# Decoder block in one kernel: where self-attention's exp and row sums, the rounding factors and the layer norms are computed

## The chip, the cores and the metric

The kernel runs on one core of a Trainium2 chip. The metric is the device time of one execution in microseconds (us), lower is better; the median of 3 runs is given. The engines are named as in the profile: PE is TensorE (matmuls and transposes; PEld is its loading of weights), DVE is VectorE, ACT is ScalarE, POOL is GpSimd, SP issues DMAs. Each engine takes its own instructions strictly in the order of its queue and waits on semaphores; SBUF is the on-chip memory, PSUM the eight banks into which PE writes.

## What is computed

A decoder block over x of shape (8, 256, 256): 8 batch elements of 256 tokens, width 256. Three parts follow one another, each with a layer norm ahead and a residual add behind:

```
x = x + attention(layernorm(x))              # causal, 8 heads of 128, 2 latent KV groups of width 32
x = x + cross_attention(layernorm(x), ctx)   # 16 heads of 16 over 77 context tokens, then relu MLP 256-512-256
x = x + ffn(layernorm(x))                    # two "bit linear" layers 256-1024-256 with exact gelu between

def bitlinear(x, w, b):
    xn = x * rsqrt(mean(x**2) + 1e-6)
    scale = 127 / clip(max(abs(xn)), 1e-5)             # per token
    xq = clip(round(xn * scale), -128, 127) / scale
    wq = ternary weights, scaled by mean(abs(w))
    return xq @ wq.T + b
```

In self-attention the probabilities are softmax(q k / sqrt(128)) with a causal mask, per head.

## The kernel before

The kernel works batch element by batch element (i = 0 to 7, on lines that the profile shows as counts of 8), each of two tiles of 128 tokens. For each element the same steps run, in groups: `sp` (layer norm, transposes and projections for self-attention), `sa` (scores, softmax numerators), `so` (weighted sum, output projection, residual), `xp`, `xs`, `xo`, `xm` (the same for cross-attention and its MLP), `f1` and `f2` (the two quantised layers), and `pro`, the one-time preparation of weights.

The work of several elements overlaps, and every engine's order is written out by hand: the table `ORDER` lists the steps of each engine, the calls at the end of each engine's function repeat it, and `Steps` turns a step's place into the semaphore count to wait for. PSUM has two uses. Four of its eight banks form `quad`, one single buffer for scores; each fill of it (self-attention's first query tile "A" with 128 keys, its second "B" with 256 keys, cross-attention's two tiles) must be emptied before the next fill. The other four are a ring that all other results of PE pass through, in PE's order.

Self-attention for one element, before:

- PE fills quad with the scores of 8 heads (`sa_scores`, L1784 to L1789; all heads share 32-wide latent keys, in 4 row groups and 2 columns c).
- DVE takes the negated maximum (`sa_max`, L1225) and adds it to the scores on the way to `a_sA` or `a_sB` in SBUF (`sa_sub`, L1235). This empties quad.
- PE transposes the differences (`sa_tr`, L1804: 2 banks for A, 4 for B), and ACT applies exp with the score's scale as it copies them to `a_p` (`sa_exp`, L821).
- PE computes the weighted sum with the values and, by a second set of matmuls with a tile of ones, the row sums spread over 32 rows (`so_pv`, L1822).
- DVE turns the sums: a stream transpose in blocks of 32 (L1244), a reciprocal of 8 columns (L1246), a transpose back (L1248), then the product (`so_y`, L1251). PE projects it (L1730) and DVE adds the residual (L1255).

A layer norm before takes its statistics on DVE (L1200, L1203), the inverse deviation on POOL (L518, L520), and on POOL also the normalisation, two instructions of 128x256 (`normalise`, L526). A rounding factor (`f1_quant`, `f2_quant` on POOL) is 127 over the guarded maximum: after DVE's maximum (L1325, L1350) POOL multiplies it by the inverse root mean square, clamps it, takes the power -1 and multiplies again (L568 to L575, L609 to L617), and DVE rounds with the factor (L1331, L1357).

ACT also applies gelu and exp from different tables: where it changes between them, a table load stands in its queue (ACT_TABLE_LOAD).

## Time and profile before

| | |
|---|---|
| median of 3 runs | 319.96 us (319.79 to 321.28) |
| the profiled execution | 321.1 us |
| its span, first to last instruction | 319.2 us |
| mean granted TensorE clock | 0.984 of full speed |
| DMA | 12.54 MB, nearly all in the first 33 us |

The profile gives for each engine the time in which it had an instruction under way ("busy"), and for each idle gap what ended it. An idle gap of an engine that sets no one's pace costs nothing; so the views by stretch of time and by group of instructions are read together. PE's matmuls overlap, so the busy time of a group is less than its count times the mean duration of one, and the pace is the distance from one to the next.

### The profile page before, as it was taken

The page shows a single profiled execution, that of the slowest core. Times are in us where ns is not written, and L with a number is a line of the kernel's source. Part 1 is how long each engine was busy: PE and PEld are TensorE (multiplying, and loading weights), DVE is VectorE, ACT ScalarE, POOL GpSimd, SP SyncE. Part 2 cuts the span into 40 slices and gives each one's busy share as a digit, 9 for nine tenths or more (in the row PEclk, how much of TensorE's full clock was granted, in tenths as well). Part 3 has the DMA queues.
Part 4 walks back from the last instruction along what each step waited for, and adds up shares of the span by engine and source line. Part 5 has one row for each costly group of instructions (what it writes and reads, how often), then busy time and mean ns, then how long its engine had stood idle before and what let it go on. Part 6 is the DMA issues. An engine that isn't in the chain of part 4 may idle for free.

```text
span 319.2 us, 8883 instructions
## 1 busy us (share of the span) xinstructions
PE 302.6 (95%) x3185; PEld 248.8 (78%) x3198; DVE 273.2 (86%) x488; ACT 191.0 (60%) x369; POOL 161.5 (51%) x315
## 2 busy tenths in 40 slices
PE   8798999999999999999999999999999999998756
PEld 8476787879888887897788878887887888786534
DVE  2228996898989799999999999989999998999973
ACT  3164435436247759478966854497445965776852
POOL 7337006282933523671778266306660485077873
PEclk9899999999999999999999999999999999999978
DMA  7999000000000000000001010000000010000011
GB/s 200 340 368 330 6 3 0 2 2 0 4 2 2 3 0 2 3 0 2 2 3 34 3 35 2 2 0 4 16 18 2 2 37 2 0 3 33 3 34 66
DMA packets 11954, 12.54 MB, mean 39 GB/s; under 512 B 1668, under 2 KB 11144, under 8 KB 11912
## 3 DMA queue, kind: packets, MB, share of 16 engines
q1 hardware_dynamic: 10648, 11.40, 10.9%
q10 hardware_dynamic: 1264, 0.59, 0.7%
q8 instruction: 26, 0.43, 0.6%
q14 instruction: 16, 0.13, 0.1%
HBM read 9.89 MB, written 2.10 MB: 38 GB/s over the span
## 4 chain that ended last, share of the span: by engine, by line
PE 77%; issue 6%; DVE 6%; POOL 5%; ACT 5%; DVEq 0%; POOLq 0%; ACTq 0%
PE bank L1724 8%; PE bank L1871 7%; PE bank L1804 6%; PE bank L1894 6%; PE bank L1822 6%; PE bank L1903 5%; PE quad L1784 4%; PE bank L1885 4%; PE bank L1730 4%; PE quad L1861 3%; PE bank L1942 3%; PE bank L1757 3%; PE bank L1718 2%; PE bank L1923 2%; PE bank L1932 2%
## 5 line engine op out<-in xcount | busy, mean ns | idle before, releaser
L845 ACT ACTIVATE c_p<-bank 77x512 f32<-77x512 f32 x64 | 35.7, 591 | 26.4 <-PE bank L1871 26.2
L1871 PE MATMUL bank<-ident,c_s 128*77 128x128 f32 x256 | 34.8, 274 | 0.4 <-DVE f_o L1369 0.4
L564 POOL TENSOR_SCALAR f_s<-f_mv 128x1 f32<-128x1 f32 x16 | 3.5, 220 | 62.0 <-DVE f_s L1325 61.4
L821 ACT ACTIVATE a_p<-bank 128x512 f32<-128x512 f32 x48 | 27.3, 601 | 10.5 <-PE bank L1804 10.1
L1894 PE MATMUL bank<-c_y,xw_s 128*128 128x128 f32 x256 | 31.5, 276 | 0.8 <-DVE c_y L1303 0.8
L1871 PEld LDWEIGHTS bank<-ident,c_s 128*77 128x77 f32 x256 | 29.5, 148 | 3.1 <-issue 1.0
L1894 PEld LDWEIGHTS bank<-c_y,xw_s 128*128 128x128 f32 x256 | 30.1, 192 | 1.3 <-issue 0.9
L1903 PE MATMUL bank<-xw_s,c_h 128*128 128x256 f32 x128 | 30.5, 381 | 0.0
L1273 DVE TENSOR_REDUCE c_nm<-quad 128x16 f32<-128x1232 f32 x16 | 23.0, 1436 | 4.2 <-PE quad L1861 4.1
L1903 PEld LDWEIGHTS bank<-xw_s,c_h 128*128 128x128 f32 x128 | 23.3, 190 | 3.6 <-ACT c_h L854 0.5
L1284 DVE TENSOR_TENSOR c_s<-quad,c_nm 128x616 f32<-128x616 f32 x32 | 24.5, 792 | 1.3
L1342 DVE SCALAR_TENSOR_TENSOR f_h<-bank,f_s,fb_s 128x512 f32<-128x512 f32 x32 | 23.0, 739 | 1.7 <-PE bank L1923 0.9
L526 POOL TENSOR_SCALAR a_xn<-xres,a_mv,a_rs 128x256 f32<-128x256 f32 x16 | 20.4, 1280 | 6.8 <-PE bank L1718 6.3
L854 ACT ACTIVATE c_h<-bank,xb_s 128x128 f32<-128x128 f32 x64 | 18.3, 372 | 6.5 <-PE bank L1894 6.3
L897 ACT ACTIVATE f_hT<-bank 128x1024 bf16<-128x1024 f16 x16 | 16.3, 1020 | 7.2 <-PE bank L1932 7.2
L884 ACT ACTIVATE f_h<-f_h 128x1024 f32<-128x1024 f32 x16 | 16.7, 1054 | 6.0 <-DVE f_h L1342 6.0
L526 POOL TENSOR_SCALAR c_xn<-xres,c_mv,c_rs 128x256 f32<-128x256 f32 x16 | 19.5, 1226 | 0.7
L1235 DVE TENSOR_TENSOR a_sB<-quad,a_nmB 128x1024 f32<-128x1024 f32 x16 | 19.2, 1214 | 0.5
L1350 DVE TENSOR_REDUCE f_s<-f_h 128x1 f32<-128x1024 f32 x16 | 19.3, 1206 | 0.0
L1225 DVE TENSOR_REDUCE a_nmB<-quad 128x8 f32<-128x2048 f32 x8 | 18.3, 2287 | 0.9 <-PE quad L1789 0.9
L1200 DVE BATCH_NORM_STATS2 a_st<-xres 128x6 f32<-128x256 f32 x16 | 6.0, 414 | 15.2 <-DMA xres<-in_x 14.5
L1942 PE MATMUL bank<-t,f_hT 128*128 128x256 bf16 x128 | 18.3, 291 | 0.6 <-ACT f_hT L897 0.3
(139 smaller groups left out, 769.8 us busy)
## 6 DMA issues: line engine op xcount, KB each, us to landing
out<-f_o SPq DMA_DIRECT2D x16, 128.0 KB, 1.7
xres<-in_x SPq DMA_DIRECT2D x1, 1536.0 KB, 10.0
c_p<-in_wqT SPq DMA_DIRECT2D x2, 512.0 KB, 6.9
c_p<-in_wo SPq DMA_DIRECT2D x1, 1024.0 KB, 9.6
f_h<-in_fw1T SPq DMA_DIRECT2D x1, 1024.0 KB, 12.1
c_s<-in_fw2T SPq DMA_DIRECT2D x1, 1024.0 KB, 11.3
xw_s<-in_xw SPq DMA_DIRECT2D x2, 512.0 KB, 9.7
fb_s<-in_fb SPq DMA_DIRECT2D x1, 512.0 KB, 6.3
```

The costliest lines, as they stand in the source:

```text
L526: nc.gpsimd.tensor_scalar(xn[:, t, :], xtile(i, t), mv[:, t, 0:1], rs[:, t:t + 1], ALU.subtract, ALU.mult).then_inc(g.sem["pool"], 1)
L821: nc.scalar.activation(dst, src, ACT.Exp, scale=SCALE_SA).then_inc(sa.sem["act"], 1)
L845: nc.scalar.activation(c_p[0:M, :, qt * P:(qt + 1) * P].rearrange("p (c j g) t -> p c j g t", c=KC, g=Q2)[:, :, j, :, :], bank("xs", f"tr{ ...
L1273: nc.vector.tensor_reduce(c_nm[:, qt, :, :], quad[:, :, 0:Q4 * M].rearrange("p j (g m) -> p j g m", m=M), axis=AX, op=ALU.max, negate=True ...
L1284: nc.vector.tensor_tensor(c_s[:, qt, j, :, :], quad[:, j, 0:Q4 * M].rearrange("p j (g m) -> p j g m", m=M), c_nm[:, qt, j, :].unsqueeze(3) ...
L1342: nc.vector.scalar_tensor_tensor(f_h[:, t, hf * 512:(hf + 1) * 512], bank("f1", f"l1_{n}", i)[:, :], f_s[:, 7, t:t + 1], fb1_s[:, hf * 512 ...
L1350: nc.vector.tensor_reduce(f_s[:, 11, t:t + 1], f_h[:, t, :], axis=AX, op=ALU.max, apply_absolute_value=True).then_inc(f2.sem["dve"], 1)
L1724: last = mm(dst[:, m * T:(m + 1) * T], w[:, c, m * P:(m + 1) * P], xT[:, c, :], start=c == 0, stop=c == KC - 1)
L1871: last = nc.tensor.transpose(dst[0:M, g * P:(g + 1) * P], c_s[:, qt, j, g, :], ident[:, :])
L1894: last = mm(bank("xm", f"w1{t}", i)[:, m * P:(m + 1) * P], xw1_s[:, c, m * P:(m + 1) * P], c_y[:, t, c, :], start=c == 0, stop=c == KC - 1)
L1903: last = mm(bank("xm", f"w2{t}", i)[:, 0:D], c_h[:, m, t * P:(t + 1) * P], xw2_s[:, m, :], start=m == 0, stop=m == MC - 1)
L1942: last = mm(bank("f2", f"l2{t}", i)[:, 0:D], f_hT[:, t, c, :], t2[:, c, :], start=c == 0, stop=c == FC - 1)
```

## The change

In words:

- Self-attention's exp moves ahead of the transpose. ACT reads quad, adds the negated maximum as its bias, applies exp, writes `a_sA` or `a_sB`, and keeps the sum of each row (`accum_out`) in `a_sum`: per element 8 instructions of 128 columns and 8 of 256. The score's scale goes into the projection `wqk` once. DVE's subtraction is gone; quad is now emptied by ACT's eight exps.
- The transposed numerators are copied to `a_p` plainly (`sa_copy`), by ACT in all six cases.
- The matmuls with ones are gone. DVE takes the reciprocal of the sums, broadcast to 32 columns per head (`sa_inv`: 256 elements per partition, one for A and one for B), PE transposes them (`so_rd`: four of 128x128), ACT copies them to `a_rd`, and DVE multiplies.
- The normalisation of both layer norms ahead of the attentions moves from POOL to DVE.
- The rounding factor: POOL prepares eps over the inverse root mean square beside the maximum; after the maximum, DVE takes the larger of the two over 127 and its reciprocal (two instructions on 128x1). Six POOL instructions per tile become three for the first layer's factor, and likewise for the second's.
- The order of all engines is a new one. ACT has 16 table loads in it, where it had 20.

The core of the diff (the order tables and the lists of calls left out):

```diff
@@ ScalarE
-            def sa_exp(i, u, n):
-                act.wait_ge(*sa.after("pe", f"tr{u}{n}", i))
...
-                nc.scalar.activation(dst, src, ACT.Exp, scale=SCALE_SA).then_inc(sa.sem["act"], 1)
+            def sa_exp(i, u, r):
+                nm, s, w = (a_nmA, a_sA, P) if u == "A" else (a_nmB, a_sB, T)
+                qt = 0 if u == "A" else 1
+                act.wait_ge(*sa.after("dve", f"mx{u}", i))
+                act.wait_ge(*sa.after("pe", f"tr{u}{r // 2 if u == 'A' else r}", i - 1))
+                act.wait_ge(*sa.after("dve", f"inv{u}", i - 1))
+                for c in range(KC):
+                    nc.scalar.activation(s[:, r, c, :], quad[:, r, c * w:(c + 1) * w], ACT.Exp, bias=nm[:, r, c:c + 1],
+                                         accum_out=a_sum[:, qt, c, r:r + 1]).then_inc(sa.sem["act"], 1)
+            def sa_copy(i, u, n):
+                act.wait_ge(*sa.after("pe", f"tr{u}{n}", i))
...
+                nc.scalar.activation(dst, src, ACT.Copy).then_inc(sa.sem["act"], 1)
+            def so_rd(i):
...
+                copied(so, "so", "rd", i, flat(a_rd))
@@ VectorE
-                nc.vector.tensor_tensor(s[:, r, :, :], quad[:, r, 0:KC * w].rearrange("p r (c m) -> p r c m", c=KC),
-                                        nm[:, r, :].unsqueeze(3).to_broadcast([P, 2, KC, w]), op=ALU.add).then_inc(sa.sem["dve"], 1)
+            def sa_inv(i, u):
...
+                nc.vector.reciprocal(a_r[:, qt, :, :, :], a_sum[:, qt, :, :].unsqueeze(3).to_broadcast([P, KC, 4, L])).then_inc(sa.sem["dve"], 1)
-                nc.vector.transpose(a_t[:, c, :, :].rearrange("p b t -> p (b t)"), src[:, T:2 * T]).then_inc(O, 1)
-                nc.vector.reciprocal(a_r[:, c, :], a_t[:, c, :, 0]).then_inc(O, 1)
-                nc.vector.transpose(a_rd[:, c, :, :], a_r[:, c, :].unsqueeze(2).to_broadcast([P, NB, 32])).then_inc(O, 1)
+            def normalise(g, i, mv, rs, xn):
...
+                for t in range(TT):
+                    nc.vector.tensor_scalar(xn[:, t, :], xtile(i, t), mv[:, t, 0:1], rs[:, t:t + 1],
+                                            ALU.subtract, ALU.mult).then_inc(g.sem["dve"], 1)
+                nc.vector.tensor_scalar(f_s[:, 13, t:t + 1], f_s[:, 11, t:t + 1], f_s[:, 12, t:t + 1], 1.0 / QMAX, ALU.max, ALU.mult).then_inc(F, 1)
+                nc.vector.reciprocal(f_s[:, 15, t:t + 1], f_s[:, 13, t:t + 1]).then_inc(F, 1)
@@ TensorE
-                for off in (0, T):
-                    for t in range(TT):
-                        for r in range(4):
-                            w = ones[:, 0:L] if off else v[:, t, group(r) * L:(group(r) + 1) * L]
+                for t in range(TT):
+                    for r in range(4):
+                        last = mm(dst[r * L:(r + 1) * L, t * P:T], v[:, t, group(r) * L:(group(r) + 1) * L], a_p[:, c, r, 2 * t:2 + t, :],
+                                  start=t == 0, stop=t == TT - 1)
+            def so_rd(i):
...
+                        last = nc.tensor.transpose(bank("so", "rd", i)[:, c * T + qt * P:c * T + (qt + 1) * P], a_r[:, qt, c, :, :].rearrange("p r l -> p (r l)"), ident[:, :])
```

How the change moves the order, at three places. PE, element 0's weighted sum, before and then after (L1822 and L1903 are `so_pv`, L1915 is `so_rd`):

```order
L1822 MATMUL bank<-a_p,a_v 32x256 x4
L1822 MATMUL bank<-a_p,a_v 32x128 x4
L1822 MATMUL bank<-a_p,ones 32x256 x4
L1822 MATMUL bank<-a_p,ones 32x128 x4
L1822 MATMUL bank<-a_p,a_v 32x256 x4
L1822 MATMUL bank<-a_p,a_v 32x128 x4
L1822 MATMUL bank<-a_p,ones 32x256 x4
L1822 MATMUL bank<-a_p,ones 32x128 x4
```
```order
L1870 MATMUL quad<-a_k,a_q 128x256 x8
L1875 MATMUL quad<-mask,identb 128x2x128 x4
L1903 MATMUL bank<-a_p,a_v 32x256 x4
L1903 MATMUL bank<-a_p,a_v 32x128 x4
L1915 MATMUL bank<-ident,a_r 128x128 x4
L1903 MATMUL bank<-a_p,a_v 32x256 x4
L1903 MATMUL bank<-a_p,a_v 32x128 x4
```

Sixteen matmuls with ones went, twice, and four transposes of the reciprocals came; element 1's second scores now stand ahead of them.

ACT around element 0's softmax, before and then after (L821 the old exp; L771 the new exp, L780 the plain copy, the other lines copies of projections; L878 and L843 touch the exp table):

```order
L781 ACTIVATE a_v<-bank 128x128
L781 ACTIVATE a_xT<-bank 128x512
L781 ACTIVATE a_q<-bank 128x512
L821 ACTIVATE a_p<-bank 128x2x2x128 x2
L781 ACTIVATE a_k<-bank 128x256
L801 ACTIVATE a_k<-bank 64x256
L821 ACTIVATE a_p<-bank 128x2x256 x4
```
```order
L771 ACTIVATE a_sA,a_sum<-quad,a_nmA 128x128 x8
L734 ACTIVATE a_k<-bank 128x256
L754 ACTIVATE a_k<-bank 64x256
L734 ACTIVATE a_q<-bank 128x512
L883 ACTIVATE kbd<-bank,part 128x4x77 x2
L876 ACTIVATE wvo<-bank 128x512
L734 ACTIVATE a_xT<-bank 128x512
L780 ACTIVATE a_p<-bank 128x2x2x128
L843 ACTIVATE junk<-mhalf 128x1
L771 ACTIVATE a_sB,a_sum<-quad,a_nmB 128x256 x8
L780 ACTIVATE a_p<-bank 128x2x256
```

The exps now stand ahead of the copies to a_p, eight in a row for each fill of quad, and what PE waits for (copies of projections) stands between them.

DVE around the same element's sums, before and then after (L1246 the old reciprocal, L1287 the new one):

```order
L1244 STREAM_TRANSPOSE a_t<-bank 128x256
L1246 RECIPROCAL a_r<-a_t 128x8
L1248 STREAM_TRANSPOSE a_rd<-a_r 128x256
L1251 TENSOR_TENSOR a_y<-bank,a_rd 128x256
L1244 STREAM_TRANSPOSE a_t<-bank 128x256
L1246 RECIPROCAL a_r<-a_t 128x8
L1248 STREAM_TRANSPOSE a_rd<-a_r 128x256
L1251 TENSOR_TENSOR a_y<-bank,a_rd 128x256
```
```order
L1287 RECIPROCAL a_r<-a_sum 128x256
L1237 BN_STATS a_st<-xres 128x6 x2
L1240 BN_AGGR a_mv<-a_st 128x2 x2
L1277 TENSOR_REDUCE a_nmB<-quad 128x8
L1302 TENSOR_TENSOR a_y<-bank,a_rd 128x256 x2
```

The two chains of four instructions behind the weighted sum became one product each; the reciprocal, 256 wide, now stands ahead of the weighted sum.

## Rows read from the trace of the kernel before

**Rows 1.** The page, part 1: each engine's busy us (share of the span) xinstructions.
```profile
PE 302.6 (95%) x3185; PEld 248.8 (78%) x3198; DVE 273.2 (86%) x488; ACT 191.0 (60%) x369; POOL 161.5 (51%) x315
```

**Rows 2.** Stretch, length, then busy us of PE, PEld, DVE, ACT, POOL; clock, DMA.
```profile
160.00:250.00 90.00, 88.85 (x1015) 74.74 (x1022) 85.15 (x149) 57.20 (x110) 43.25 (x91) 1.00 0.03 11
60.00:300.00 240.00, 236.14 (x2624) 198.47 (x2636) 224.49 (x405) 157.18 (x305) 125.32 (x255) 1.00 0.02 7
255.00:319.20 64.20, 53.75 (x515) 43.47 (x516) 53.83 (x98) 41.34 (x78) 39.52 (x98) 0.95 0.07 22
```

**Rows 3.** Timeline of PE: start us, us, work; in element 0's weighted sum.
```profile
37.51 0.83 PE L1822 MATMUL bank<-a_p,ones 128*32 128x256 f32 x16
38.16 0.83 PE L1822 MATMUL bank<-a_p,a_v 128*32 128x256 f32 x16
```

**Rows 4.** Groups by line: instruction, count | busy us, mean ns | idle us before, releaser.
```profile
L821 ACT ACTIVATE a_p<-bank 128x512 f32<-128x512 f32 x48 | 27.3, 601 | 10.5 <-PE bank L1804 10.1
...
L1235 DVE TENSOR_TENSOR a_sB<-quad,a_nmB 128x1024 f32<-128x1024 f32 x16 | 19.2, 1214 | 0.5
...
L854 ACT ACTIVATE c_h<-bank,xb_s 128x128 f32<-128x128 f32 x64 | 18.3, 372 | 6.5 <-PE bank L1894 6.3
...
L1822 PE MATMUL bank<-a_p,ones 128*32 128x256 f32 (+1 forms) x256 | 13.3, 326 | 0.0
...
L526 POOL TENSOR_SCALAR a_xn<-xres,a_mv,a_rs 128x256 f32<-128x256 f32 x16 | 20.4, 1280 | 6.8 <-PE bank L1718 6.3
...
L1804 PE MATMUL bank<-ident,a_sB 128*128 128x128 f32 x128 | 18.1, 275 | 0.1
...
L1235 DVE TENSOR_TENSOR a_sA<-quad,a_nmA 128x512 f32<-128x512 f32 x16 | 10.4, 682 | 0.3
...
L1248 DVE STREAM_TRANSPOSE a_rd<-a_r 128x256 f32<-128x256 f32 x16 | 7.1, 446 | 0.6
...
L1244 DVE STREAM_TRANSPOSE a_t<-bank 128x256 f32<-128x256 f32 x16 | 7.0, 438 | 0.7 <-PE bank L1822 0.5
...
L836 ACT ACTIVATE c_q<-bank,xbq_s 128x256 f32<-128x256 f32 x16 | 6.7, 472 | 6.7 <-PE bank L1724 6.7
...
L1322 DVE TENSOR_SCALAR f_c<-xres,f_mv 128x256 f32<-128x256 f32 x16 | 5.7, 353 | 0.6
...
L871 ACT ACT_TABLE_LOAD x5 | 6.4, 1283 | 0.1
...
L1297 DVE RECIPROCAL c_r<-c_t 128x16 f32<-128x16 f32 x16 | 3.9, 241 | 0.2
...
L1382 DVE RECIPROCAL winv<-wmean 128x2 f32<-128x2 f32 x1 | 0.2, 165 | 0.0
...
L891 ACT ACTIVATION_READ_ACCUMULATOR f_sq<-f_h 128x1 f32 x16 | 3.3, 205 | 0.0
...
L1246 DVE RECIPROCAL a_r<-a_t 128x8 f32<-128x8 f32 x16 | 3.3, 203 | 0.5
```

**Rows 5.** Two stretches, ACT's instructions on tile a_p alone: length, busy us (count).
```profile
160.00:250.00 90.00, 10.47 (x18) 1.00 0.03 11
20.00:140.00 120.00, 15.11 (x28) 1.00 0.11 37
```

**Rows 6.** A stretch, instructions on quad alone: PE, PEld, DVE busy (x).
```profile
20.00:140.00 120.00, 20.84 (x316) 13.66 (x316) 54.84 (x49) 1.00 0.11 37
```

**Rows 7.** Timeline, element 0's first scores and their maximum.
```profile
20.60 0.61 PE L1787 MATMUL quad<-mask,identb 128*128 128x256 bf16 x4
21.72 0.75 DVE L1200 BATCH_NORM_STATS2 a_st<-xres 128x6 f32<-128x256 f32 x2 [7.48 <-DMA xres<-in_x]
22.62 1.23 DVE L1225 TENSOR_REDUCE a_nmA<-quad 128x8 f32<-128x1024 f32 x1
```

**Rows 8.** Timeline, the last tile's rounding factor on POOL and its use.
```profile
311.13 0.20 POOL L609 TENSOR_TENSOR f_s<-f_s 128x1 f32<-128x1 f32 x1
312.58 0.75 DVE L1357 TENSOR_SCALAR f_hq<-f_h,f_s 128x1024 f16<-128x1024 f32 x1 [1.05 <-POOL f_s L617]
```

More of the change, by code:

```diff
@@ L906, in pro_wqk @@
                 nc.scalar.activation(wqk[:, :, c * P:(c + 1) * P], bank("pro", f"wqk{c}")[:, 0:D].rearrange("p (m n) -> p m n", m=KC),
[L907 removed]
+                                     ACT.Copy, scale=SCALE_SA).then_inc(pro.sem["act"], 1)
             def pro_wvo():
@@ new lines, in _ @@
+            sa_exp(3, "A", 0)
+            xm_relu(0, 1)
+            sa_copy(2, "B", 2)
+            sa_exp(3, "A", 3)
+            sa_exp(3, "A", 2)
+            so_rd(2)
+            xm_relu(0, 0)
+            sp_q(4)
+            sp_k(4)
+            sa_copy(3, "A", 1)
+            xs_exp(1, 0, 0)
+            xs_exp(1, 1, 0)
+            xs_exp(1, 1, 1)
+            xs_exp(1, 0, 1)
+            xs_exp(1, 1, 3)
+            xs_exp(1, 0, 3)
+            xs_exp(1, 1, 2)
+            sa_exp(3, "B", 3)
@@ new lines, in _ @@
+            f1_gelu(0, 1)
+            sp_v(5)
+            sa_copy(4, "B", 1)
+            sa_exp(5, "A", 0)
+            sa_exp(5, "A", 2)
+            sa_exp(5, "A", 3)
+            sa_copy(4, "A", 1)
+            sa_exp(5, "A", 1)
+            sp_q(6)
+            sa_copy(4, "B", 3)
+            sa_copy(4, "B", 0)
+            sa_copy(4, "B", 2)
+            f1_qT(1, 1)
+            f2_ssq(0, 0)
+            so_rd(4)
+            f1_qT(1, 0)
+            f2_ssq(0, 1)
+            xm_relu(2, 1)
@@ new lines, in _ @@
+            sa_exp(5, "B", 3)
+            xp_xT(3)
+            sa_exp(5, "B", 2)
+            sa_exp(5, "B", 1)
+            sa_exp(5, "B", 0)
+            xp_q(3)
+            f1_gelu(1, 0)
+            f2_hT(0, 0)
+            f1_gelu(1, 1)
+            sa_copy(5, "A", 0)
+            f2_ssq(1, 1)
+            f1_pre(1)
+            sa_copy(5, "A", 1)
+            xm_relu(2, 0)
+            f2_hT(0, 1)
+            f1_pre(2)
+            xs_exp(3, 0, 1)
+            sa_copy(5, "B", 3)
+            sa_copy(5, "B", 1)
@@ new lines, in _ @@
+            xp_xT(4)
+            xs_exp(3, 0, 2)
+            f2_ssq(1, 0)
+            f1_qT(2, 1)
+            xs_exp(3, 0, 0)
+            xp_q(4)
+            sa_copy(5, "B", 0)
+            xs_exp(3, 0, 3)
+            xs_exp(3, 1, 2)
+            xs_exp(3, 1, 3)
+            f2_hT(1, 1)
+            f1_qT(2, 0)
+            f2_hT(1, 0)
+            xs_exp(3, 1, 1)
+            xs_exp(3, 1, 0)
+            sp_k(6)
+            so_rd(5)
+            sa_copy(5, "B", 2)
+            f2_pre(4)
@@ L1238, in so_y, with sa_copy @@
+            @element
+            def sa_copy(i, u, n):
+                dve.wait_ge(*sa.after("pe", f"tr{u}{n}", i))
+                for c in range(KC):
+                    dve.wait_ge(*so.after("pe", f"pv{c}", i - 1))
+                dst, src = transposed_scores(i, u, n)
+                nc.vector.tensor_copy(dst, src).then_inc(sa.sem["dve"], 1)
             @element
             def so_y(i, c):
-                O = so.sem["dve"]
-                src = bank("so", f"pv{c}", i)
                 dve.wait_ge(*so.after("pe", f"pv{c}", i))
-                dve.wait_ge(*so.after("dve", f"y{c}", i - 1))
@@ new lines, in _ @@
+            f2_hmax(4, 0)
+            xm_resid(5, 1)
+            xo_y(6, 0)
+            xs_sub(7, 1, 0)
+            f1_stat(5, 1)
+            xo_T(6, 1)
+            xs_sub(7, 1, 1)
+            f1_centre(5, 1)
+            xo_y(6, 1)
+            f2_out(3, 0)
+            f2_hq(4, 0)
+            f1_q(5, 1)
+            xm_resid(6, 0)
+            f1_h(5, 1)
+            f1_stat(6, 0)
+            f1_h(5, 0)
+            f2_hq(4, 1)
+            xo_T(7, 0)
+            f1_centre(6, 0)
+            f1_h(5, 3)
@@ L2218, in _ @@
+            sa_scores(6, "B")
+            xp_xT(5)
+            xs_tr(4, 0, 0)
+            f1_qT(3, 0)
+            xs_tr(4, 0, 3)
+            xp_q(5)
+            f2_l2(1, 1)
+            xo_pv(4, 1)
+            xo_pv(4, 0)
+            sa_tr(6, "B", 3)
+            sa_tr(6, "B", 0)
+            f1_l1(3, 1)
+            sa_tr(6, "B", 2)
+            xs_scores(5, 0)
+            f2_hT(2, 0)
+            sa_tr(6, "B", 1)
+            f1_qT(3, 1)
+            sp_q(7)
             sa_tr(6, "A", 0)
```

1951 lines of the change are left out of this document (955 added, 996 removed).

## The prediction

> **What bounds the kernel now.** I read the engines' busy times first. PE is busy 302.6 of 319.2 us, DVE 273.2, ACT 191.0, POOL 161.5 [rows 1]. A share over the span says little, so the second view is the same busy time cut into stretches. From 60 to 300 us PE is busy 236.1 of 240 us and DVE 224.5 of 240, while ACT has 157.2 [rows 2]. So PE sets the pace, DVE follows it with about 15 us of slack, and ACT spends a third of the time idle; in the groups by line most of that idle time ends on PE, as the 10.5 us before the a_p group [rows 4]. In the last 64.2 us PE and DVE have 53.8 us each [rows 2]: there neither is full, and the chains between them count.
>
> The sum is made against the profiled execution: 321.1 us, of which 319.2 is its span. The median of the runs is 319.96 us, 1.1 us lower, and I give the forecast on that scale. A measurement of this kernel tells about 0.5% (1.6 us) from no change.
>
> **Part 1: the sums leave PE.** The row sums of self-attention are made today by matmuls with a tile of ones: 256 of them, in 16 blocks of 16. One block follows the other after 0.65 us (37.51 to 38.16) [rows 3]. Sixteen blocks are 10.4 us; the group's busy time of 13.3 us [rows 4] is longer, because the ends of neighbouring blocks overlap. In their place stand four transposes of 128x128 f32 for each batch element, 32 in all. The nearest row is the transposes of a_sB, 18.1 us for 128, or 0.141 us each [rows 4]: 4.5 us. Net on PE: **-5.9 us**. All else on PE (projections, transposes of the scores, cross-attention, the two quantised layers) stays as it is in number and shape. As PE is the engine without slack, I count this saving in full.
>
> **Part 2: ACT takes the exp before the transpose.** Before, VectorE subtracted the maximum and ACT applied exp as it copied the transposed scores out (48 instructions, 601 ns) [rows 4]. These 48 stay, as plain copies of the same shape, and cost the same. New are 128 exps straight from quad with a bias from memory, 64 of 128 columns and 64 of 256, each followed by a read of the accumulator.
> - 128 columns: the ReLU group has this width and a bias from memory, 18.3 us for 64, or 0.286 us each when they follow one another [rows 4].
> - 256 columns: the group of c_q, 6.7 us for 16, or 0.419 us each [rows 4].
> - The accumulator's read takes 0.205 us [rows 4], the row that ACT's sum of squares already shows.
> - Together 64 x 0.491 + 64 x 0.624 = 71.4 us, and 8 copies of the reciprocals at 0.6 us make it 76.2.
> If the accumulator's read ends the overlap of neighbours, the units are 0.577 and 0.677 us (372 and 472 ns plus 205) and the sum is 85; if the read hides beside the next instruction it is 50. I take 76, since the rows of the sum of squares show the read as time of its own. ACT's order has 16 table loads where it had 20, at 1.283 us each [rows 4]: -5.1 us. ACT: 191.0 + 76.2 - 5.1 = 262 us, 84% of a span of 313.
>
> Is there room where it is added? From 160 to 250 us ACT is busy 57.2 us [rows 2], with 18 of the 48 instructions on a_p [rows 5]. The added work comes in the same proportion: 18/48 x 76.2 = 28.6 us, in all 86 of 90 us (89 of 90 with the dearer units). So it fits, with little left. An engine that full serves its queue late: something that PE waits for stands behind other work. I charge **+2 us**, between 0 and the case of its own below.
>
> **Part 3: DVE.** It loses both subtractions (19.2 and 10.4 us), the two stream transposes around the old reciprocal (7.0 and 7.1) and that reciprocal (3.3): -47.0 us [rows 4]. It gains:
> - 32 normalisations of 128x256, like the centring of f_c at 353 ns: 11.3 us [rows 4].
> - 64 tiny instructions (the guarded maximum and its reciprocal, for two roundings and 16 tiles). The smallest reciprocal takes 165 ns [rows 4]: 10.6 us.
> - 16 reciprocals over 256 elements. No row shows one so wide. For 2, 8 and 16 elements the rows have 165, 203 and 241 ns [rows 4]: 6.3 and then 4.75 ns more per element. Carried to 256 this is 1.38 to 1.77 us; I take 1.55, which is 24.8 us. The lower bound is one pass over 256 elements, 0.35 us as f_c, or 5.6 us in all.
> DVE comes to 273.2 - 47.0 + 11.3 + 10.6 + 24.8 = 273 us: unchanged. Its 15 us of slack between 60 and 300 take in PE's saving of 6 and leave 9. I charge nothing.
>
> A rule speaks against the wide reciprocals. The Trainium skill (VectorE: DVE Perf Modes, section "First, the fixed hardware budget") says that a reciprocal runs an iterative divide with a repeat count of 8. Read as eight passes at the 1.04 ns per element of the subtractions (1214 less 682 ns for 512 elements more), a wide one would be about 2.2 us, an estimate, and DVE 283 us. The slopes in the rows are 4.6 to 6.1 such passes, so the trace bears it out in kind and less in size.
>
> **Part 4: POOL, and the latencies.** POOL loses the normalisations, 1280 ns each (two per layer norm) [rows 4], and most of the scalar chains. It isn't near any bound, so the work itself is worth nothing; what counts is that a layer norm takes two passes of 0.35 us on DVE instead of 2.4 on POOL. In the middle PE has other work queued and that hides it. At two places nothing hides:
> - Start. The first scores end at 21.2 us, but their maximum starts at 22.62, since DVE's queue holds it behind statistics which wait for a DMA until 21.72 [rows 7]. The new order puts the maximum ahead of those. At most 1.4 us; PE fills part of this time already, so **-1 us**.
> - End. The last tile's rounding factor passes four POOL instructions after its maximum, from 311.13 to 312.58, 1.45 us [rows 8]. Now two DVE instructions of 0.165 us do it, and this for two tiles in a row: **-1 us** for the last, the one before it lies beside the other.
>
> **Sum.** -5.9 - 1 - 1 + 2 = -5.9 us: 315.2 on the profiled execution, **314.0 us** on the scale of the median.
>
> **The rivals.**
> *A, the forecast.* PE stays the bound and keeps most of its saving: 311 to 317.5, as the charge for ACT goes from 0 to 5.5. For it: PE without slack. Chance 0.48.
>
> *B, more than PE's saving.* The new order also removes idle time that the old latencies left. PE was idle 3.9 us between 60 and 300, and 10.4 in the last 64.2 us [rows 2]. With ACT's charge gone and a third of this taken out, 14.3/3 = 4.8: 314 - 2 - 4.8 = 307. Against it: three engines now stand near 90%. Chance 0.17.
>
> *C, DVE becomes the bound.* The wide reciprocals cost 2.2 us. DVE's 283.5 us need its idle time to shrink; outside 60 to 300 it has 79.2 - 48.7 = 30.5 us idle, set by the loads and the last chains. 283.5 + 30.5 + 3 for short waits = 317 span, 317.8 on the median's scale. The skill's rule on the reciprocal names this case. Against it stand the measured slopes. Chance 0.15.
>
> *D, slower: quad is held too long.* Self- and cross-attention share one score buffer. A fill is free again after the maximum and the subtraction; now after the maximum and eight exps on ACT. From 20 to 140 us PE's and DVE's work on quad is 75.7 of 120 us [rows 6]. In the new form a pair of fills has 8 exps of each width, 8.9 us, where the subtractions took 3.8 (2 x 0.682 + 2 x 1.214): 5.1 us more. 28 of the 48 instructions on a_p fall in this stretch [rows 5], so 28/48 x 8 = 4.7 such pairs: 24 us more, 100 of 120. The 20 us left are 1.05 us for each of some 19 fills, and a fill needs three hops between engines plus whatever stands ahead of the exps on ACT (a copy of 0.6 us, or a table load of 1.28). It decides from the point where this wait passes 1.05 us. With 0.6 us beyond it, over 16 fills: +9.6, or 323.6 us. For it: ACT's load in part 2. Chance 0.20.
>
> **How the numbers follow.** Faster by over 0.5% (under 318.4): 0.46 of A, 0.17 of B and 0.07 of C, whose 317.8 lies near that edge: 0.70. Within 0.5%: 0.02 of A, 0.08 of C and 0.02 of a mild D: 0.12. Slower (over 321.6): the other 0.18 of D. The range that leaves out about 0.2 runs from 306.5 (B with its whole idle share) to 322.5 (D at half its price and somewhat more). With both ends of the reciprocal (0.35 us frees DVE, which brings B; 1.77 us adds 3.5 us to DVE, inside its slack) and ACT's 50 or 85 us it still holds.
>
> **What would show each step.** Right: PE's busy time falls by about 6 us to 297; 32 transposes of a_r and no matmul with ones; ACT's exps near 0.49 and 0.62 us with their reads and ACT near 262 us; the reciprocal between 1.4 and 1.8 us; DVE near 273. In stretches PE still shows 19.5 or more of 20 us in the middle. D would show as PE idle on quad, waiting for ACT, between 20 and 140 us; C as PE idle with DVE over 19.5 of 20; B as less than 10 us of idle PE in the last 64. The forecast is wrong if PE has gaps of over 3 us in sum in the middle that end on ACT, or if the copies to a_p got dearer with the new load.

## The result, and the profile after

The changed kernel takes 331.2 us (median of 4 runs, 328.7 to 333.1) against 320.6 us of the kernel before on the same chip: ratio 1.033, 95% interval 1.024 to 1.041. It is **slower by 10.5 us**, where I had forecast 314.0 us, 6 us faster.

The page of the kernel after, part 1 (busy us, share of the span, instructions) and the granted clock in 40 slices, with the answer that it gives in place of [rows 1]; its span is 330.3 us:

```profile
PE 302.2 (91%) x2961; PEld 243.5 (74%) x2974; DVE 278.7 (84%) x519; ACT 241.9 (73%) x629; POOL 93.7 (28%) x187
PEclk9999999799999999999999999997999999999959
```

PE's busy time has hardly moved (302.6 to 302.2), and the span is 11.1 us longer: PE's idle time went from 16.6 to 28.1 us. That the busy time didn't fall, though 224 matmuls went, has to do with the slices at 7 and 5 in the clock's line. The stretches of after, with the columns of [rows 2]:

```profile
60.00:300.00 240.00, 228.44 (x2419) 188.59 (x2424) 216.04 (x404) 185.98 (x472) 64.37 (x131) 0.99 0.02 6
266.10:330.30 64.20, 53.75 (x515) 43.01 (x518) 57.38 (x126) 43.39 (x77) 26.02 (x61) 0.95 0.07 24
```

From 60 to 300 us PE is idle for 11.6 us where it was 3.9. In the last 64.2 us it is busy for 53.75 us, exactly as before, so the loss doesn't lie there. DVE, which I had called unchanged, shows *less* busy time in the middle (216.0 against 224.5 us); judged by such sums, it has more slack than ever.

Who ends PE's waits (engine, place, releaser: us in all, times, longest):

```profile
PE quad L1870 <- DVE c_s L1335: 3.3, 2, 2.2
PE bank L2024 <- DVE f_hq L1428: 2.6, 3, 1.1
PE bank L1915 <- DVE a_r L1287: 2.0, 2, 1.6
PE bank L2004 <- DVE f_q L1394: 1.8, 2, 1.3
PE bank L2015 <- DVE xres L1360: 1.7, 1, 1.7
PE bank L1804 <- DVE a_xn L1257: 1.6, 1, 1.6
```

These are the six longest sums. In the whole list DVE ends 20.6 us of PE's waits and ACT 2.7; before, DVE ended 7.6. DVE's are of many kinds: scores of cross-attention, rounding, the reciprocals, a residual, a norm. I read this as an in-order queue that runs late as a whole. The groups of after that are new or that answer to [rows 4]:

```profile
L1287 DVE RECIPROCAL a_r<-a_sum 128x256 f32<-128x256 f32 x16 | 27.6, 1738 | 0.0
...
L771 ACT ACTIVATE a_sB<-quad,a_nmB 128x256 f32<-128x256 f32 x64 | 29.5, 488 | 1.6 <-DVE a_nmB L1277 1.6
...
L780 ACT ACTIVATE a_p<-bank 128x512 f32<-128x512 f32 x48 | 27.7, 605 | 8.4 <-PE bank L1891 8.3
...
L771 ACT ACTIVATE a_sA<-quad,a_nmA 128x128 f32<-128x128 f32 x64 | 22.7, 378 | 3.9 <-DVE a_nmA L1277 3.3 <-issue 0.5
...
L771 ACT ACTIVATION_READ_ACCUMULATOR a_sB<-quad,a_nmB 128x1 f32 x64 | 14.2, 221 | 0.0
...
L1915 PE MATMUL bank<-ident,a_r 128*128 128x128 f32 x32 | 5.4, 296 | 2.1 <-DVE a_r L1287 2.0
```

The longest of PE's waits, in the timeline of after (start us, us, work, idle before it and its releaser), DVE and PE only:

```profile
219.36 3.35 DVE L1287 RECIPROCAL a_r<-a_sum 128x256 f32<-128x256 f32 x2
...
222.63 1.38 DVE L1324 TENSOR_REDUCE c_nm<-quad 128x16 f32<-128x1232 f32 x1
...
222.85 0.60 PE L1963 MATMUL bank<-ident,c_s 128*77 128x128 f32 x4
...
224.14 1.51 DVE L1335 TENSOR_TENSOR c_s<-quad,c_nm 128x616 f32<-128x616 f32 x2
...
225.70 1.24 PE L1870 MATMUL quad<-a_k,a_q 32*128 32x128 f32 x16 [2.25 <-DVE c_s L1335]
```

Two wide reciprocals stand back to back, 3.35 us. Behind them in DVE's queue stand cross-attention's maximum and subtraction, which have to empty quad before PE can fill it again. PE runs out of other work and idles for over 2 us. The granted clock then falls as well. Three stretches of after, columns as above, the clock third from the right:

```profile
58.20:61.60 3.40, 3.40 (x32) 2.32 (x34) 2.91 (x4) 1.09 (x2) 0.00 (x0) 0.50 0.00 0
225.50:228.90 3.40, 3.20 (x23) 2.60 (x24) 2.23 (x3) 0.82 (x3) 0.00 (x0) 0.50 0.00 0
314.20:321.00 6.80, 5.94 (x33) 3.48 (x30) 6.27 (x12) 5.18 (x8) 3.12 (x7) 0.50 0.05 16
```

After this wait, and after one of 1.6 us that ended at 57.97, PE works at the lower level of 1.2 GHz for 3.4 us each; a longer stretch of it lies at the end. In them PE is busy for 12.5 us, about twice what that work takes at 2.4 GHz (the four transposes of the reciprocals at 58.70 us take 0.99 us to the next step; the same four in e1_narrow, at 2.4 GHz, 0.53): 6.3 us are lost. The kernel before had two such stretches, with 8.9 us of PE's busy time, or 4.4 us lost:

```profile
13.30:16.70 3.40, 3.40 (x10) 2.50 (x10) 0.94 (x4) 0.78 (x3) 2.18 (x4) 0.50 1.11 341
...
306.80:313.70 6.90, 5.48 (x35) 4.20 (x36) 4.57 (x8) 4.14 (x5) 4.55 (x13) 0.51 0.18 58
```

These stretches aren't the same in every execution of a kernel. The four of after had mean granted clocks of 0.979 (the profiled one, 332.2 us), 0.988, 0.985 and 0.998 (328.7 us). So with nearly the full clock the changed kernel is 3.5 us faster than in its profile, and still 8 us slower than the kernel before: most of the loss isn't the clock.

### The profile page after: what moved, and what is told of

It reads as the page before. It is cut to its first block and busy times, and to the rows that moved or that the text cites. A ratio compares the mean times of both kernels' runs of the same rounds, so it can differ in the third digit from the quotient of the medians.

```text
span 330.3 us, 8756 instructions
## 1 busy us (share of the span) xinstructions
PE 302.2 (91%) x2961; PEld 243.5 (74%) x2974; DVE 278.7 (84%) x519; ACT 241.9 (73%) x629; POOL 93.7 (28%) x187
## 5 line engine op out<-in xcount | busy, mean ns | idle before, releaser
L810 ACT ACTIVATE c_p<-bank 77x512 f32<-77x512 f32 x64 | 35.6, 590 | 15.4 <-PE bank L1963 15.1
L780 ACT ACTIVATE a_p<-bank 128x512 f32<-128x512 f32 x48 | 27.7, 605 | 8.4 <-PE bank L1891 8.3
L771 ACT ACTIVATE a_sB<-quad,a_nmB 128x256 f32<-128x256 f32 x64 | 29.5, 488 | 1.6 <-DVE a_nmB L1277 1.6
L1287 DVE RECIPROCAL a_r<-a_sum 128x256 f32<-128x256 f32 x16 | 27.6, 1738 | 0.0
L771 ACT ACTIVATE a_sA<-quad,a_nmA 128x128 f32<-128x128 f32 x64 | 22.7, 378 | 3.9 <-DVE a_nmA L1277 3.3
L1277 DVE TENSOR_REDUCE a_nmB<-quad 128x8 f32<-128x2048 f32 x8 | 18.3, 2287 | 5.9 <-PE quad L1875 5.9
L819 ACT ACTIVATE c_h<-bank,xb_s 128x128 f32<-128x128 f32 x64 | 18.3, 370 | 5.7 <-PE bank L1986 5.6
L1891 PE MATMUL bank<-ident,a_sB 128*128 128x128 f32 x128 | 18.2, 275 | 3.3 <-DVE f_h L1405 1.5
L2015 PE MATMUL bank<-t,f_qT 128*128 128x512 bf16 x51 | 15.8, 399 | 5.0 <-DVE xres L1360 1.7
```

The source lines that it names most:

```text
L771: nc.scalar.activation(s[:, r, c, :], quad[:, r, c * w:(c + 1) * w], ACT.Exp, bias=nm[:, r, c:c + 1], accum_out=a_sum[:, qt, c, r:r + 1]). ...
L780: nc.scalar.activation(dst, src, ACT.Copy).then_inc(sa.sem["act"], 1)
L810: nc.scalar.activation(c_p[0:M, :, qt * P:(qt + 1) * P].rearrange("p (c j g) t -> p c j g t", c=KC, g=Q2)[:, :, j, :, :], bank("xs", f"tr{ ...
L1287: nc.vector.reciprocal(a_r[:, qt, :, :, :], a_sum[:, qt, :, :].unsqueeze(3).to_broadcast([P, KC, 4, L])).then_inc(sa.sem["dve"], 1)
L2015: last = mm(bank("f1", f"l1_{n}", i)[:, :], f_qT[:, c, t * P:(t + 1) * P], t1[:, c, hf * 512:(hf + 1) * 512], start=c == 0, stop=c == KC - 1)
```

## The experiments

All twelve were timed in 3 rounds beside the kernel before (320.9, 322.0 and 321.3 us in the three sets). "us against before" is the ratio less 1, times 321, and the differences between experiments below are taken in it; such a difference is uncertain by 1.5 to 2 us, one against after by 3. PE's idle time is the span less PE's busy time in the profiled execution.

| kernel | ratio, interval | us against before | PE busy / idle | DVE busy |
|---|---|---|---|---|
| before | 1 | 0 | 302.6 / 16.6 | 273.2 |
| after | 1.033 (1.024 to 1.041) | +10.5 | 302.2 / 28.1 | 278.7 |
| e1_narrow | 0.985 (0.981 to 0.989) | -4.8 | 294.2 / 19.3 | 261.8 |
| e3_no_sums | 1.027 (1.022 to 1.031) | +8.6 | 302.4 / 28.0 | 278.6 |
| e4_norm_pool | 1.069 (1.064 to 1.074) | +22.2 | 303.5 / 35.6 | 265.3 |
| e5_factor_pool | 1.072 (1.067 to 1.077) | +23.2 | 305.7 / 38.7 | 269.1 |
| e7_load_kept | 1.013 (1.009 to 1.017) | +4.0 | 299.3 / 26.1 | 275.8 |
| e8_bcast | 0.987 (0.983 to 0.990) | -4.3 | 300.0 / 15.0 | 255.8 |
| e9_load_spread | 1.002 (0.999 to 1.004) | +0.5 | 300.3 / 19.9 | 272.0 |
| e10_spread_pool | 0.986 (0.981 to 0.991) | -4.6 | 296.5 / 16.8 | 255.3 |
| b1_wide_before | 1.079 (1.073 to 1.085) | +25.3 | 309.9 / 33.7 | 296.6 |
| b2_norm_dve | 1.014 (1.011 to 1.017) | +4.6 | 303.0 / 20.9 | 283.4 |
| b3_factor_dve | 1.031 (1.025 to 1.036) | +9.8 | 307.7 / 21.7 | 284.2 |
| b4_load_before | 1.037 (1.032 to 1.042) | +11.7 | 304.0 / 25.5 | 287.2 |

### The wide reciprocals alone: e1_narrow

```diff
-                nc.vector.reciprocal(a_r[:, qt, :, :, :], a_sum[:, qt, :, :].unsqueeze(3).to_broadcast([P, KC, 4, L]))
+                nc.vector.reciprocal(a_ri[:, qt, :, :], a_sum[:, qt, :, :])
+                nc.vector.tensor_copy(a_r[:, qt, :, :, :], a_ri[:, qt, :, :].unsqueeze(3).to_broadcast([P, KC, 4, L]))
```

> The changed kernel with one edit: the reciprocal is taken of the 8 sums alone (a new tile a_ri of 8 columns), and a plain copy spreads it to 256 columns. Expected durations on DVE 0.20 us and 0.42 us where one instruction took 1.74 us: DVE loses 16 x 1.1 = 18 us of work. Theory V (PE's new waits are waits for a DVE that is full or busy with a long instruction): 8 to 14 us faster than the changed kernel's 331, that is 317 to 323. Theory Q (the score buffer quad is held by ACT's eight exps, and all engines wait along): under 3 us faster, 328 or more. Theory O (the new order of the engines leaves PE waiting whatever the durations): also under 3 us.

It takes 315.75 us: 15.3 us less than the changed kernel (uncertain by 3), more than the 8 to 14 of theory V, and 1.5% faster than the kernel before. The edit also lets ACT's next exps go ahead once the short reciprocal has read the sums. The page of e1_narrow, part 1 and the clock, its stretch from 60 to 300 us, and its timeline at the place shown above:

```profile
PE 294.2 (94%) x2961; PEld 239.3 (76%) x2974; DVE 261.8 (84%) x535; ACT 241.0 (77%) x629; POOL 94.1 (30%) x187
PEclk9999999999999999999999999999999999999999
```
```profile
60.00:300.00 240.00, 233.03 (x2453) 193.09 (x2458) 217.26 (x451) 193.44 (x487) 76.74 (x156) 1.00 0.03 8
```
```profile
208.42 0.29 DVE L1279 COPY a_r<-a_ri 128x256 f32<-128x256 f32 x1
...
208.86 0.29 DVE L1279 COPY a_r<-a_ri 128x256 f32<-128x256 f32 x1
...
209.07 1.43 DVE L1316 TENSOR_REDUCE c_nm<-quad 128x16 f32<-128x1232 f32 x1
...
210.63 1.50 DVE L1327 TENSOR_TENSOR c_s<-quad,c_nm 128x616 f32<-128x616 f32 x2
...
211.69 0.60 PE L1955 MATMUL bank<-ident,c_s 128*77 128x128 f32 x4
```

The pair of reciprocals takes 0.9 us in place of 3.35, and PE finds its next work in time. The 16.8 us between the two spans split into 8.8 of idle PE (28.1 to 19.3) and 8.0 of PE's busy time (302.2 to 294.2), of which the half-speed stretches explain 6.3. That split holds for these two executions only. The other three of e1_narrow had mean clocks of 0.984 to 0.995, and between the executions with the fullest clock (after at 0.998, e1_narrow at 1.0) the gap is 13.4 us. So of the 15.3 us some 2 are the clock's and the rest is waiting. Nor does a wait always bring the clock down: e1_narrow's page has a wait of 1.9 us at the same norm, which ends at 56.07 us, and keeps the full clock behind it.

So the wide reciprocals are the cause of the loss, and the rest of the change is a gain of some 5 us.

### Load or latency: e7_load_kept

```diff
+                nc.vector.reciprocal(a_rj[:, qt, :, :, 0:20], a_ri[:, qt, :, :].unsqueeze(3).to_broadcast([P, KC, 4, 20]))
```

> e1_narrow (reciprocal of 8 sums, then a copy that spreads them: 315.8 us) with the time that it saved on VectorE put back behind it: after each copy a reciprocal over 160 elements of an unused tile, about 1.15 us, on which nobody waits. VectorE's busy time is that of the changed kernel again, but the sums are ready as early as in e1_narrow. Theory V (VectorE's time, whoever needs the result): 328 to 333 us, as the changed kernel. Theory L (the transposes of the reciprocals wait for the long instruction itself): 315 to 319 us.

Between both: 326.2 us, or (by the ratios) 8.8 us over e1_narrow and 6.5 under the changed kernel. The group of the added work in e7_load_kept, and the same pair in its timeline:

```profile
L1283 DVE RECIPROCAL a_rj<-a_ri 128x160 f32<-128x160 f32 x16 | 18.3, 1144 | 0.0
```
```profile
217.22 1.14 DVE L1283 RECIPROCAL a_rj<-a_ri 128x160 f32<-128x160 f32 x1
...
218.67 1.14 DVE L1283 RECIPROCAL a_rj<-a_ri 128x160 f32<-128x160 f32 x1
219.73 1.38 DVE L1320 TENSOR_REDUCE c_nm<-quad 128x16 f32<-128x1232 f32 x1
```

Nobody waits for this work, and it costs 8.8 us all the same: the maximum stands behind it, and PE waits 2.8 us for quad behind cross-attention's subtraction, where e1_narrow waits 0.2. Neither theory holds by itself: some 9 of the 15 us are VectorE's time as such. The other 6 come with the rest of the difference, a reciprocal that PE's transposes wait for and 3 us more of DVE time; the run doesn't part these two.

### The same load in small pieces: e9_load_spread

```diff
+                nc.vector.reciprocal(a_rj[:, n, :], a_one[:, :]).then_inc(sa.sem["dve"], 1)
```

Here the added work is 22 elements of a constant, 64 times at even distances along DVE's queue.

> e1_narrow plus the same sum of unused work as e7_load_kept (18 us), but in 64 pieces of 0.28 us (22 elements) spread evenly over VectorE's queue in place of 16 of 1.14 us. If the sum of VectorE's time counts: 325 to 328 us, as e7_load_kept (326.2). If it is the length of one block, in which a result that TensorE needs stands behind it: 318 to 322 us.

321.8 us, in the range for the length of one block. 64 pieces of 276 ns are 17.7 us of work and cost 5.3 us against e1_narrow; 16 pieces of 1144 ns are 18.3 us and cost 8.8. Load costs something even in small pieces, and more in large ones: 0.30 us for each us, against 0.48. The two runs differ in two things, the length of a piece and its place in the queue (even distances, or behind each copy), and don't part them. Part of the 5.3 is the clock again: at the same mean clock of 0.989 the gap between the two kernels is about 4.5 us.

### Is the kernel before free to take load? b4_load_before and b1_wide_before

b4 adds the same line, with 160 elements, twice per batch element behind `so_y` in the kernel before. b1 lengthens the reciprocal that is there:

```diff
-                nc.vector.reciprocal(a_r[:, c, :], a_t[:, c, :, 0]).then_inc(O, 1)
+                nc.vector.reciprocal(a_r[:, c, :, :], a_t[:, c, :, :]).then_inc(O, 1)
```

> The kernel before, plus work on VectorE on which nobody waits: behind each product of the weighted sum a reciprocal over 160 elements of a constant into an unused tile, 16 x 1.15 = 18.4 us. This is the step of my prediction that failed, taken alone (slack of 15 us between 60 and 300 us takes in added work). Slack theory: 320 to 325 us. Theory V, load at the slope of b1_wide_before (25 us for 24.6, but there the long instruction also stood in the chain to the output projection): 339 us. At the slope of e7_load_kept (9 us for 18 put back, as load alone): 328 to 332 us, which I take as likeliest.

> The kernel before, with one thing from the change put in: the reciprocal of the turned sums is taken of all 256 columns (16 instructions of about 1.74 us) where it was taken of 8 (0.20 us), and the transpose behind it reads the 256 columns. That adds 16 x 1.54 = 24.6 us to VectorE, nothing to any other engine. My prediction's reading (VectorE had 15 us of slack between 60 and 300 us which takes in added work): 24.6 - 15 = 10 us or less, 326 to 331 us. Theory V (work on VectorE delays the chains that TensorE waits on, slack or not; e1_narrow took 18 us of it away and got 15.5 back, 0.85 us per us): 24.6 x 0.85 = 21, so 338 to 345 us.

b4: 18.3 us of work with no consumer cost 11.7 us, as taken for likeliest and far from the 0 to 4 of the slack theory. The kernel took in 6.6 us of it; the 15 us of slack of my prediction don't exist as a reserve. b1: 24.8 us of work in the chain cost 25.3 us, one for one, and more than theory V's 17 to 24. Its page, part 1, and two of PE's waits:

```profile
PE 309.9 (90%) x3185; PEld 251.5 (73%) x3198; DVE 296.6 (86%) x488; ACT 191.3 (56%) x369; POOL 160.2 (47%) x315
```
```profile
PE bank L1717 <- DVE a_y L1238: 6.9, 3, 2.6
PE bank L1919 <- DVE a_y L1238: 4.5, 2, 2.4
```

Before, the reciprocal stands in a chain that holds two banks of the ring until `a_y` is written, so PE waits at whatever comes next in the ring (L1717 is the output projection, L1919 a matmul of the quantised layers). Not all of the 25.3 us is waiting: of the 7.3 us that PE is busy longer, about 5 is half speed (estimated from the mean clock, 0.970 against 0.984). In the changed kernel the reciprocal stands ahead of the weighted sum. There the wide form costs 15.3 us over a narrow form with 18.3 us less work (1738 less 195 and 400 ns, 16 times), or 0.84 us for each us, against 1.02 here. With uncertainties of 3 and 2 us this doesn't show that the new place softens it.

### Still less on VectorE: e8_bcast and e10_spread_pool

```diff
-                        last = nc.tensor.transpose(bank("so", "rd", i)[:, c * T + qt * P:c * T + (qt + 1) * P], a_r[:, qt, c, :, :].rearrange("p r l -> p (r l)"), ident[:, :])
+                        for r in range(4):
+                            last = mm(bank("so", "rd", i)[r * L:(r + 1) * L, c * T + qt * P:c * T + (qt + 1) * P],
+                                      a_ri[:, qt, c, r:r + 1].to_broadcast([P, L]), ident[:, :])
```

> The changed kernel with the reciprocal of 8 sums only and no spreading on VectorE at all: TensorE spreads them, by 16 matmuls of a broadcast column (128x32) with the identity for each element where 4 transposes of 128x128 stood. VectorE loses 16 x (1.74 - 0.2) = 24.6 us against the changed kernel, and 6 us against e1_narrow. TensorE's part costs about the same (16 small matmuls took 0.65 us in the kernel before, these have 128 columns each, and 4 transposes 0.56 us). Theory V: 315.8 - 0.85 x 6 = 310.7, so 309 to 313 us. If TensorE is the bound once the long reciprocals are gone: 315 to 317 us.

e10 keeps the copy and gives it to GpSimd:

```diff
-                nc.vector.tensor_copy(a_r[:, qt, :, :, :], a_ri[:, qt, :, :].unsqueeze(3).to_broadcast([P, KC, 4, L]))
+                nc.gpsimd.tensor_copy(a_r[:, qt, :, :, :], a_ri[:, qt, :, :].unsqueeze(3).to_broadcast([P, KC, 4, L]))
```

> e1_narrow with the copy that spreads the reciprocals over 256 columns on GpSimd, which is idle 70% of the time. VectorE loses 6.4 us more; the chain from the sums to their transposes gets longer by a hop and by a slower copy (about 1.2 us for 256 columns against 0.40). By load (e8_bcast: 3 us less waiting for 6 us less on VectorE): 312 to 314 us. By latency, as e4_norm_pool and e5_factor_pool, which lost 12 us each by a move to GpSimd: 318 to 325 us.

Both took a further 6 us off DVE and both are as fast as e1_narrow, not faster. e10 missed both its ranges with 315.6 us; e8, 317.5 us or 316.7 by the ratio, is near the one for TensorE as the bound. So the price of a us on DVE isn't a constant; the last 6 us, spread over 16 short steps, are worth nothing that can be seen. In e8 PE's idle time does fall (19.3 to 15.0 us), but PE has more to do. The group of e8_bcast shows it, to be held against 5.4 us for 32 transposes:

```profile
L1903 PE MATMUL bank<-ident,a_ri 128*32 128x128 f32 x256 | 8.6, 275 | 0.0
```

My expectation had counted 16 matmuls for each element; the trace has 32. e10 has 2.5 us less idle time and 2.3 us more PE busy time, at a mean clock of 0.989 where e1_narrow's profiled execution had 1.0; the runs of e1_narrow at 0.989 and 0.984 took 316.1 and 317.7 us, so e10 may be better by a fraction of a us, which these runs can't show. The latency that GpSimd adds to this chain cost nothing that can be seen in the time (PE waits 1.6 us for it in all).

### ACT's part: e3_no_sums

```diff
-                    nc.scalar.activation(s[:, r, c, :], quad[:, r, c * w:(c + 1) * w], ACT.Exp, bias=nm[:, r, c:c + 1],
-                                         accum_out=a_sum[:, qt, c, r:r + 1])
+                    nc.scalar.activation(s[:, r, c, :], quad[:, r, c * w:(c + 1) * w], ACT.Exp, bias=nm[:, r, c:c + 1])
```

The sums are left out and stand at a constant 1.0.

> The changed kernel without the accumulated sums: the exps have no accumulator output and so no read of it, and the sums are a constant of 1.0 (the division by the row sums is left out, everything else runs as it did). ACT loses 128 reads of 0.22 us, of which neighbours overlap; each fill of quad is held about 1.0 to 1.7 us less. Theory Q: 8 or more us faster, 323 or less, with the gain between 20 and 140 us and PE's waits for quad gone. Theory V: DVE's work is the same, 0 to 3 us faster, 328 to 331. Theory O: 0 to 3 us.

ACT loses 11.4 us of busy time (241.9 to 230.5) and eight exps of 128 columns are through 0.75 us sooner (one follows the other after 0.25 us, where it was 0.34). PE's idle time stays at 28.0 us, and the time at 330.1 us is within the spread of the changed kernel. This run leaves the exps themselves in place; that they aren't what holds PE up is shown by e1_narrow, which has all 128 of them with their reads, ACT at 241.0 us, and is faster than the kernel before. So rival D falls.

### Norms and factors, each moved alone

e4 puts the norms back on GpSimd in the changed kernel, e5 the two instructions of each factor. b2 and b3 make the same moves forwards in the kernel before. Each step is put into its new engine's order where the other had run it in time. The lines of e4, and in reverse of b2:

```diff
-                    nc.vector.tensor_scalar(xn[:, t, :], xtile(i, t), mv[:, t, 0:1], rs[:, t:t + 1], ALU.subtract, ALU.mult)
+                    nc.gpsimd.tensor_scalar(xn[:, t, :], xtile(i, t), mv[:, t, 0:1], rs[:, t:t + 1], ALU.subtract, ALU.mult)
```

> The changed kernel with one part undone: the normalisations of both layer norms are back on POOL, each put into POOL's queue at the place that its time in the trace gives. DVE loses 32 x 0.41 us and what blocked it, 13 to 16 us; the layer norm gets 1.7 us longer. Theory V: 4 to 10 us faster than the changed kernel, 321 to 327. Theories Q and O: within 2 us of it, or slower by the longer chain.

> The kernel before, with only the layer norms' application moved from GpSimd (32 x 1.28 us) to VectorE (32 x 0.35 = 11.3 us), each put into VectorE's order at the time at which it ran on GpSimd. By VectorE's load alone (0.85 us per us): +9.6, 328 to 332 us. By latency (e4_norm_pool, which put them back on GpSimd in the new kernel, cost 12 us): the shorter step outweighs the load, 312 to 320 us. If in this order other work covers the longer step, as the prediction held, and the slack takes the load in: 319 to 322.

The lines of e5 (the first layer's; the second's likewise); b3 puts the removed two in place of the old form:

```diff
-                nc.vector.tensor_scalar(f_s[:, 4, t:t + 1], f_s[:, 2, t:t + 1], f_s[:, 3, t:t + 1], 1.0 / QMAX, ALU.max, ALU.mult)
-                nc.vector.reciprocal(f_s[:, 6, t:t + 1], f_s[:, 4, t:t + 1])
+                nc.gpsimd.tensor_scalar(s1(4, t), s1(2, t), s1(3, t), 1.0 / QMAX, ALU.max, ALU.mult)
+                nc.gpsimd.tensor_tensor(s1(6, t), s1(4, t), mhalf[:, TT:TT + 1], op=ALU.pow)
```

> The changed kernel with one part half undone: the guarded maximum and its reciprocal (the power -1) are two instructions on POOL instead of two on DVE, for both roundings. DVE loses 64 instructions, 11.7 us; the factor comes 0.5 us later, 32 times. Theory V: 3 to 8 us faster, 323 to 328, less what the longer chain costs in the last 30 us (about 1 us). Theories Q and O: no gain, 331 to 333.

> The kernel before, with only the rounding factors in the new form: guarded maximum and reciprocal as two instructions on VectorE (64 x 0.165 = 10.6 us) where four or three on GpSimd stood behind the maximum. By load alone at 0.5 us per us: +5, 324 to 327 us. By latency (e5_factor_pool, two GpSimd instructions in their place in the new kernel, lost 12 us): the shorter chain gives back more, 312 to 319 us.

Against the changed kernel, moving either back costs 12 to 13 us though DVE has 10 to 13 us less to do, where theory V had a gain of 4 to 10 and of 3 to 8 us. Here latency outweighs load. For the norms the waits of PE in e4_norm_pool say why:

```profile
PE bank L1790 <- POOL c_xn L527: 8.7, 5, 2.2
...
PE bank L1790 <- POOL a_xn L527: 2.9, 3, 2.2
```

These are 11.6 us of waits for two passes of 1.2 us each where DVE takes two of 0.4. Moving them forwards in the old order, alone, costs 4.6 us (b2), and the factors alone 9.8 us (b3), against the gain that both expectations gave for latency; 4.6 us is half of what load alone was to cost, 9.8 twice that. I read it so that each of the two orders fits the engines for which it was made: the kernel before covers a slow norm on GpSimd with other work and can't use a fast one, the changed kernel relies on the fast one. No run with an order made anew for such a mixture shows it. For the factors the runs don't say more than that: in b3 the loss is 5.1 us of idle and 5.1 us of busy PE for 11.0 us of added DVE time (the mean clock is 0.974 against 0.984, which may be some 3 us of the busy part), and no single wait stands out.

## Why the prediction was wrong, point by point

**What bounds the kernel.** PE sets the pace, with DVE next: right. That DVE "follows it with about 15 us of slack" was the mistake from which the rest came. Idle time summed over 240 us isn't a reserve: b4 took in 6.6 us of 18.3. The idle time lies where DVE waits for PE; an added instruction can stand somewhere else, in front of a result which PE needs.

**Part 1, PE.** The matmuls with ones went and 32 transposes came, at 5.4 us of busy time for the 4.5 that I had from the distance of one to the next. With the half-speed share taken off, PE's busy time falls from 298.2 (302.6 - 4.4) to 294.2 us in e1_narrow, which has none; measured from the first weight load of each step to that of the next, the weighted sum falls from 22.2 to 11.9 us and the transposes take 4.4: 5.9 us net, as forecast. In the changed kernel's own profile it is hidden under the half-speed stretches and the waits.

**Part 2, ACT.** The exps take 378 and 488 ns and their reads 218 to 221. The reads lie beside the next instruction, as the timeline of after shows:

```profile
52.09 0.38 ACT L771 ACTIVATE a_sA<-quad,a_nmA 128x128 f32<-128x128 f32 x1
...
52.34 0.22 ACT L771 ACTIVATION_READ_ACCUMULATOR a_sA<-quad,a_nmA 128x1 f32 x1
52.44 0.38 ACT L771 ACTIVATE a_sA<-quad,a_nmA 128x128 f32<-128x128 f32 x1
```

One unit of 128 columns follows the other after 0.35 us, where I had 0.491. ACT stands at 241.9 us against my 262; the sum erred by 20 us, on the harmless side, because the reads hide, the case that I had priced at 50 us and set aside. The charge of 2 us for ACT's load is tested by no run alone; leaving out the reads gave 1.9 us, less than its uncertainty.

**Part 3, DVE: the step that failed.** Its price was nearly right: 1738 ns for a wide reciprocal, at the top of my range of 1.38 to 1.77 and above the 1.55 that I took; DVE in all 278.7 us for 273. Read as in the prediction, the repeat count of 8 that the Trainium skill gives (VectorE: DVE Perf Modes, section "First, the fixed hardware budget") would have made it 2.2 us, an estimate. The measurement lies between it and my 1.55, and decides. What failed is the sentence "I charge nothing". The same load put into the kernel before costs 11.7 us as dead weight (b4) and 25 us in the chain (b1); in the changed kernel the wide form costs 15.3 us over the narrow one (e1). That term alone turns the gain into the loss: with the narrow form the changed kernel takes 315.75 us, near the 314.0 forecast. That DVE's sum stayed almost the same was no comfort: what left it were steps of 0.2 to 1.2 us, and 27.6 us came back in 16 steps of 1.74, at places two in a row. That the same load costs less in short steps is what e9 against e7 shows, with the change of place that goes with it.

**Part 4.** The start did move: the first maximum of self-attention begins 4.2 us earlier than in [rows 7]. Nothing of it is left after 60 us. The line of after in the timeline, and the first 60 us of before and of after (columns as in [rows 2]):

```profile
18.39 1.23 DVE L1277 TENSOR_REDUCE a_nmA<-quad 128x8 f32<-128x1024 f32 x1 [3.25 <-PE quad L1873]
```
```profile
0.00:60.00 60.00, 55.30 (x482) 42.54 (x483) 37.22 (x66) 24.78 (x52) 24.32 (x29) 0.97 0.52 166
```
```profile
0.00:60.00 60.00, 53.63 (x404) 40.91 (x408) 37.91 (x62) 39.05 (x132) 12.96 (x21) 0.99 0.52 166
```

PE has 1.7 us more idle time in them than before; one wait of 1.6 us is the norm described at the end. The steps that stand in these 60 us differ, so this is a rough reading.

The end is another matter. The last tile's maximum and its rounding, before (its rounding starts at 312.58 [rows 8]) and after:

```profile
309.57 1.21 DVE L1350 TENSOR_REDUCE f_s<-f_h 128x1 f32<-128x1024 f32 x1
```
```profile
321.86 1.21 DVE L1413 TENSOR_REDUCE f_s<-f_h 128x1 f32<-128x1024 f32 x1
...
323.81 0.75 DVE L1428 TENSOR_SCALAR f_hq<-f_h,f_s 128x1024 f16<-128x1024 f32 x1
```

From the end of the maximum to the rounding it was 1.80 us and is 0.74; from the start of that maximum to the end of the span, 9.6 us and 8.4. So the second -1 us did come where it was placed, and is lost in the sum. That in the middle other work hides a norm's latency on POOL was right for the old order (PE waits 0.3 us for it in all) and wrong for the new one (11.6 us in e4).

**The rivals.** C had the right engine by the wrong mechanism: DVE as a bound by its sum, 317.8 us at 2.2 us per reciprocal. DVE is at 84% in after, at most 19.3 of 20 us in any slice of 20 us. D had the right sign, and one place out of several, a quad that is freed late, but laid it on ACT and between 20 and 140 us; its +9.6 us gave 323.6, and 331.2 was measured. The timeline at 219 us shows DVE's reciprocals ahead of the maximum, and e1_narrow clears ACT. No case of mine let long steps on an engine with slack cost nearly their full length. The range ended at 322.5 us for the same reason: its upper end was D at half its price.

## What to carry to other kernels

Cost an instruction that is added to an in-order queue by what stands behind it there, not by the engine's share of idle time: in this kernel each us of added work with no consumer cost 0.3 us in pieces of 0.28 us, 0.5 to 0.6 in pieces of 1.1 us, and 0.8 to 1 where a consumer waited for it; 6 us taken off in short pieces gave nothing. Take an expensive function of few distinct values before the broadcast, not after it. And where PE is the bound, compare executions at the same granted clock before a busy time is read: the clock fell behind some waits of about 2 us and not behind others, and moved this kernel by 3.5 us from one execution to the next.
